# Last step of a fused GNN, attention and mixture-of-experts kernel: where gathered rows lie and when they are added, and how output tiles are stored

## What is computed

```python
topk_p, topk_i = jax.lax.top_k(probs, K)            # K = 2 of E = 8 experts for each row
dispatch = order[:, :capacity]                      # 97 rows for each expert
xg = xf[dispatch]
gate = jax.nn.silu(jnp.einsum('ech,ehi->eci', xg, rg))
up = jnp.einsum('ech,ehi->eci', xg, ru)
eout = jnp.einsum('eci,eih->ech', gate * up, rd)
w = jnp.take_along_axis(wdense.T, dispatch, axis=1)
contrib = eout * (w * valid)[..., None]
routed = jnp.zeros_like(xf).at[dispatch.reshape(-1)].add(contrib.reshape(-1, h))
shared = jax.nn.silu(x @ sg) * (x @ su) @ sd        # inner width 8192
return shared + SCALE * routed.reshape(b, s, h)
```

## Time and profile before

| what | us |
|---|---|
| median of three timed runs | 2904.63 (2904.53 to 2905.37) |
| the profiled execution | 2901.85 |
| its span, first to last instruction | 2900.1 |
| TensorE busy | 2848.7 (98%) |
| VectorE busy | 2232.1 (77%) |
| ScalarE busy | 1498.0 (52%) |
| GpSimd busy | 54.9 (2%) |
| mean granted TensorE clock | 0.993 |

### The profile page before, as it was taken

How to read it: one execution, slowest core, us unless ns; L and a number is a source line. 1 busy time by engine, 2 the same in 40 slices (tenths; PEclk the granted TensorE clock), 3 DMA queues, 4 the chain that set the end, 5 groups by cost and what they waited for, 6 DMA issues and landing times.

```text
span 2900.1 us, 43188 instructions
## 1 busy us (share of the span) xinstructions
PE 2848.7 (98%) x16148; PEld 2403.3 (83%) x16148; DVE 2232.1 (77%) x2724; ACT 1498.0 (52%) x1950; POOL 54.9 (2%) x73
## 2 busy tenths in 40 slices
PE   8999999899999999999999999999999999999997
PEld 8997899878888888888888888888888888888876
DVE  7835334888888888888888888888888888888886
ACT  7722222555555555555555555555555555555562
POOL 0100000000000000000000000000000000000001
PEclk9999999999999999999999999999999999999998
DMA  3010111366666666666666666666666666666684
GB/s 111 29 67 30 59 59 45 101 228 220 217 226 220 219 219 227 220 219 217 227 220 219 219 226 219 219 218 227 220 219 218 226 221 218 220 227 220 218 294 144
DMA packets 265789, 549.18 MB, mean 189 GB/s; under 512 B 16412, under 2 KB 82204, under 8 KB 265437
## 3 DMA queue, kind: packets, MB, share of 16 engines
q1 hardware_dynamic: 261626, 532.20, 54.1%
q0 software_dynamic: 3936, 14.06, 1.5%
HBM read 537.49 MB, written 8.70 MB: 188 GB/s over the span
## 4 chain that ended last, share of the span: by engine, by line
PE 93%; DVE 4%; ACT 1%; issue 1%; DMA 0%; SPq 0%; DVEq 0%; ACTq 0%
PE ps L1818 26%; PE ps L1822 26%; PE ps L1821 26%; PE ps L1558 3%; PE ps L1615 2%; PE ps L1613 2%; PE ps L1614 2%; PE ps L1673 2%; PE ps L1598 1%; DVE c_lo L1355 1%; PE ps L1865 1%; PE ps L1711 1%; PE ps L1709 1%; PE ps L1710 1%; DVE resid L1345 0%
## 5 line engine op out<-in xcount | busy, mean ns | idle before, releaser
L1355 DVE TENSOR_TENSOR c_lo<-raw,c_hi 128x1024 fp32r<-128x1024 f32 x832 | 985.4, 1220 | 100.7 <-ACT c_hi L764 100.4
L764 ACT CAST c_hi<-raw 128x1024 fp32r<-128x1024 f32 x832 | 863.2, 1050 | 155.1 <-PE ps L1822 152.3
L1818 PE MATMUL ps<-tok_hi,c_hi 128*128 128x314 f32 x1792 | 553.1, 309 | 8.3 <-DVE tok_lo L1247 6.4
L1822 PE MATMUL ps<-tok_hi,c_lo 128*128 128x314 f32 x1792 | 552.0, 308 | 0.0
L1821 PE MATMUL ps<-tok_lo,c_hi 128*128 128x314 f32 x1792 | 552.0, 308 | 0.0
L1818 PE MATMUL ps<-c_hi,xgT_hi 128*97 128x512 f32 x1024 | 403.6, 394 | 0.8 <-DVE xgT_lo L1412 0.8
L1822 PE MATMUL ps<-c_hi,xgT_lo 128*97 128x512 f32 x1024 | 403.2, 394 | 0.0
L1821 PE MATMUL ps<-c_lo,xgT_hi 128*97 128x512 f32 x1024 | 402.3, 393 | 0.0
L1419 DVE TENSOR_TENSOR resid<-ps,resid 125x512 f32<-125x512 f32 x320 | 218.7, 686 | 180.5 <-PE ps L1822 180.4
L1818 PEld LDWEIGHTS ps<-tok_hi,c_hi 128*128 128x128 f32 x1792 | 339.6, 189 | 11.4 <-issue 7.2
L1821 PEld LDWEIGHTS ps<-tok_lo,c_hi 128*128 128x128 f32 x1792 | 340.0, 190 | 1.4
(11 more groups left out here) (244 smaller groups left out, 3958.6 us busy)
## 6 DMA issues: line engine op xcount, KB each, us to landing
raw<-in_L_ffn_rg SPq DMA_DIRECT2D x256, 512.0 KB, 4.7
raw<-in_L_ffn_ru SPq DMA_DIRECT2D x256, 512.0 KB, 4.7
raw<-in_L_ffn_rd SPq DMA_DIRECT2D x256, 512.0 KB, 6.2
raw<-in_L_ffn_sg SPq DMA_DIRECT2D x64, 512.0 KB, 4.5
raw<-in_L_ffn_su SPq DMA_DIRECT2D x64, 512.0 KB, 5.4
raw<-in_L_ffn_sd SPq DMA_DIRECT2D x64, 512.0 KB, 5.6
wl<-in_L_mix_w_qkv SPq DMA_DIRECT2D x6, 2048.0 KB, 7.8
wl<-in_L_gnn_W SPq DMA_DIRECT2D x2, 2048.0 KB, 29.5
```

Of the source, the lines that this page charges most:

```text
L764: nc.scalar.copy(c_hi[u % RING][:], raw_at_(q, r)[:]).then_inc(sem("hi_done"), 1 + (U - UNITS) * (u == UNITS - 1))
L1355: V.tensor_tensor(c_lo[u % RING][:], raw_at_(q, r)[:], c_hi[u % RING][:].bitcast(F32), ALU.subtract).then_inc(sem("lo_done"), 1 + (U - UNI ...
L1818: m = MM(out_, l_hi, r_hi, start=first, stop=False, skip_group_check=skip)
L1822: return MM(out_, l_lo, r_hi, start=False, stop=last, skip_group_check=skip)
```

## The change

It does four things, all in the last step or behind it. (1) The gathered rows of tiles 2 to 4 go to six of the raw weight buffers, and GpSimd waits for the split that reads each buffer last (`lo_done`) and no longer for `unit_used`. (2) On VectorE `routed_add` moves into `factors()`, ahead of the splits of S1, A22 and S4. (3) The adds of gathered rows are taken one by one: (0,0) stands ahead of `shared_inner(0)`, (0,1) behind it, tiles 1 and 2 ahead of `shared_up(1)`, and tiles 3 and 4 between the shared adds, ahead of n = 2, 4, 5 and 6. (4) Each output tile leaves as two DMAs, of 112 and 13 rows; the last tile besides in two halves of 512 columns.

```diff
--- before.py
+++ after.py
@@ -321,10 +321,9 @@
     assert here() <= early_at
 
 
-    tok_at = raw_at + RAW * 4096
-    got_at = [eout_at, r_h_at, hT_at, xgT_at]
-    for b in (B11, T3, T2):
-        got_at += [tok_at + b * 8 * 4 * HW, tok_at + b * 8 * 4 * HW + 4 * 4 * HW]
+    last_raw = [raw_at + (((Q - 1) * BLK + b) % RAW) * 4096 for b in range(LAST.b0 - 2, LAST.b0 + 4)]
+    freed, factor = last_raw[:2], last_raw[2:]
+    got_at = [eout_at, r_h_at, hT_at, xgT_at] + freed + [factor[r] for r in (R_A11, R_A22, R_A21, R_A12)]
     got = [[place(f"got{c}_{t}", [P, D], F32, at=got_at[2 * t + c]) for t in range(NT)] for c in range(2)]
 
     def rw_half(i):
@@ -481,12 +480,18 @@
                 step(e, q)
         for q in range(Q):
             step(E - 1, q, LAST if q == Q - 1 else STEP)
-        for t in range(NT):
+        SPLIT = (slice(0, GROWS), slice(GROWS, TP))
+        for t in range(NT - 1):
 
             sp.wait_ge(sem("sd_added"), count(E - 1, Q - 1, 2 * NT, 2 * t + 2 + ONE))
-            sp.dma_start(out_t[t], resid[:, t, :]).then_inc(sem("out_stored"), 16)
-        sp.wait_ge(sem("out_stored"), 16 * NT)
-
+            for rows in SPLIT:
+                sp.dma_start(out_t[t, rows], resid[rows, t, :]).then_inc(sem("out_stored"), 16)
+        for half in range(2):
+            c = slice(half * HALF, (half + 1) * HALF)
+            sp.wait_ge(sem("sd_added"), count(E - 1, Q - 1, 2 * NT, 2 * (NT - 1) + half + 1 + ONE))
+            for rows in SPLIT:
+                sp.dma_start(out_t[NT - 1, rows, c], resid[rows, NT - 1, c]).then_inc(sem("out_stored"), 16)
+        sp.wait_ge(sem("out_stored"), 2 * 16 * (NT + 1))
 
     @block.gpsimd
     def _(pool):
@@ -567,9 +572,11 @@
         pool.dma_start(eout_d[E * CAP:(E + 1) * CAP, :], eout[:]).then_inc(sem("eout_stored"), 16)
         pool.wait_ge(sem("eout_stored"), 16 * (E + 1))
         for t in range(NT):
-            if t >= 2:
-                pool.wait_ge(sem("unit_used"), count(E - 1, Q - 1, U, LAST.s + t - 1 + USED0))
             for c in range(2):
+                if t >= 2:
+                    last = (LAST.s - 2, LAST.s - 1, LAST.s + F_S1, LAST.s + F_A22, LAST.s + F_S4,
+                            LAST.s + F_S4)[2 * (t - 2) + c]
+                    pool.wait_ge(sem("lo_done"), count(E - 1, Q - 1, U, U + last + 1))
                 nc.gpsimd.indirect_dma_start(
                     out=got[c][t][:], out_offset=None, in_=eout_d,
                     in_offset=bass.IndirectOffsetOnAxis(ap=pos_u[:, c, t:t + 1], axis=0)).then_inc(
@@ -1337,13 +1344,11 @@
                 r = eout[:, half * HALF:(half + 1) * HALF]
                 V.tensor_tensor(r, PS[R0 + half][0:CAP, :], r, ALU.add).then_inc(sem("rd_added"), 1)
 
-        def choices_add(t0, t1):
-
-            for t in range(t0, t1):
-                for c in range(2):
-                    dve.wait_ge(sem(f"g_in{c}_{t}"), 16)
-                    link(V.scalar_tensor_tensor(out=resid[:, t, :], in0=got[c][t][0:TP, :], scalar=wts[:, c, t:t + 1],
-                                                in1=resid[:, t, :], op0=ALU.mult, op1=ALU.add))
+        def choice_add(t, c):
+
+            dve.wait_ge(sem(f"g_in{c}_{t}"), 16)
+            link(V.scalar_tensor_tensor(out=resid[:, t, :], in0=got[c][t][0:TP, :], scalar=wts[:, c, t:t + 1],
+                                        in1=resid[:, t, :], op0=ALU.mult, op1=ALU.add))
 
         def step(e, q, order=STEP):
             def lo(u):
@@ -1358,7 +1363,7 @@
             def sums(i):
                 factor_sum(e, q, order, i)
 
-            def factors():
+            def factors(between=None):
 
                 sums(F_S3)
                 lo(order.s + F_A11)
@@ -1369,6 +1374,8 @@
                 lo(order.s + F_S2)
                 lo(order.s + F_A12)
                 sums(F_S4)
+                if between:
+                    between()
                 lo(order.s + F_S1)
                 lo(order.s + F_A22)
                 lo(order.s + F_S4)
@@ -1435,19 +1442,21 @@
                 routed_inner(1)
                 lo(23)
                 turned_lo(1)
-                factors()
-                routed_add(count(e, q, U, order.rd + 8 + USED0), cleared)
+                factors(lambda: routed_add(count(e, q, U, order.rd + 8 + USED0), cleared))
                 shared_up(0)
+                choice_add(0, 0)
                 shared_inner(0)
-                choices_add(0, 1)
+                choice_add(0, 1)
                 lo(31)
                 lo(32)
-                choices_add(1, 2)
+                for t in (1, 2):
+                    for c in range(2):
+                        choice_add(t, c)
                 shared_up(1)
                 shared_inner(1)
                 for n in range(2 * NT):
-                    if n % 2 == 0 and n >= 4:
-                        choices_add(n // 2, n // 2 + 1)
+                    if n in (2, 4, 5, 6):
+                        choice_add(*((3, 0), (3, 1), (4, 0), (4, 1))[(2, 4, 5, 6).index(n)])
                     shared_add(n)
                 return
             if order is FIRST:
```

## The result

The changed kernel takes 2887.83 us in the median of six runs (2886.5 to 2889.31), the kernel before 2904.58 (2903.06 to 2905.46). The ratio is 0.9943, 95% interval 0.9933 to 0.9952: 16.8 us less. The forecast was 2886.0, with a range of 2883 to 2891.5. The profiled execution took 2887.84 us, its span 2886.1.

A forecast was written before the change was run, and what follows sets the result against it. The slow output drain was taken to set the end, hiding VectorE's late last sum. Last sum 8.6 us earlier plus faster stores moves the span from 2900.1 to 2881.5; 2904.63 - 18.6 = 2886.0 us, range 2883 to 2891.5.

The forecast's parts named there:

- Drain by five engines, end set by it: Run's end: output stores drain at 114 GB/s, share 0.31 (5 of 16 engines), hiding VectorE's finish by 13.6 us.
- routed_add for nothing, gathers 7.17 us earlier: Last step: the routed adds fit in VectorE's 2.47 us of idle time; everything on POOL's queue moves 7.17 us forward.
- VectorE's order: Last step: adds laid out on VectorE, last sum at 2877.9 instead of 2886.5; TensorE's gap 0.4 us, full clock.
- The term that I had at 8.6 us: End of VectorE's work: last sum ready 8.6 us earlier, 2886.5 to 2877.9.
- The tail: After the last sum: final 1.02 MB at 277 GB/s takes 3.7 us, plus 0.8; end 2882.0, taken as 2881.5.
- The distance carried over: Whole run: the timed median 2904.63 lies 2.8 us above the profiled 2901.85; this distance was kept unchanged.
- Rival A: Saturated DMA stretch, last step: ScalarE late again, end 1.9 to 4.5 us later, 2888 to 2890.5; chance 0.16.
- Rival B: Final stores: last three 13-row pieces run behind the 112-row ones, end 2.1 us later, 2888.1; chance 0.05.
- C: Last step's gathers: rows land as late as now, only the drain's rate helps, 11 us less, 2893.6; chance 0.06.
- D: Final stores: 114 GB/s limits the written side, not five engines; 4.6 us less, 2900.0; chance 0.04.
- E: First gathered add: each microsecond its rows come beyond 2849.7 delays the end by one; slower, 2911; chance 0.02.

## Why the prediction was right, point by point

- *Drain by five engines, end set by it.* Right: the share was 0.31 before and 0.32 with the stores of 125 put back, 5 of 16 engines by estimate, and the two kernels that change only the store show that it set the end: tail 13.59 to 3.60 us, and back to 17.27.
- *routed_add for nothing, gathers 7.17 us earlier.* Right: no split moved (ahead of the first one 1.14 us idle are left), and GpSimd's store was issued 2.72 us behind the start of the factor sum against 9.90 before, 7.18 us earlier. Putting it back cost 8.1 us.
- *VectorE's order.* The last add 38.87 us behind the factor sum by my layout (2877.9 - 2839.03), 38.93 measured; TensorE's gap 0.31 against 0.4, the clock behind it 1.00. The term that I had at 8.6 us was 8.55 (47.48 - 38.93).
- *The tail.* This term of the sum was mis-sized: 3.6 us by my number (2881.5 - 2877.9), 5.26 in the profiled execution, 4.73 to 4.75 in three others. The working had 3.7 us for the last 1.02 MB at 277 GB/s, and 0.8 behind, which gives 2882.0; I then took 2881.5, half a microsecond less, for no reason in a row. The data themselves took from about 2880.5 to 2885.3 in the changed kernel, at 255 GB/s up to 2884.5 and at 33 and less behind. The rate of a lone tile (the stores of y) was used for two tiles in a row, one behind the other; the order with tile 3 first, in which tile 4 leaves alone, has 3.64. In the profiled execution these 1.7 us are nearly the whole distance from 2886.0 to 2887.83; with the usual tail of 4.75 they would have been 1.1.
- *The distance carried over.* I added the 2.8 us between the median and the profiled execution of the kernel before unchanged. The profile of the changed kernel took 2887.84 us, its median, and its last factor sum started 2.88 us later than in the profile before. So the carry was right: the profile before was a quick one in its untouched part.
- *Rival A* came true in part: ScalarE is late in all nine profiled executions with ten early gathers, by 1.1 to 3.3 us at worst, mostly hidden and worth 1.8 us in one. I had it at 0.16 as a case of its own; it is rather a spread on every run. The clock did not fall with it: behind the 2.15 us of standing still it was granted at 1.00, behind 6.54 us (routed_add late) at 0.50.
- *Rival B* (small pieces dear) fell. With tile 3's data out of the way the tail is 3.6 us with four pieces, two of them of 13 rows, and the last tile stored whole, with one small piece less, has 4.69 against 4.73 to 4.75.
- *Rivals C, D and E* fell: C by GpSimd's store, 7.18 us earlier, and the 0.68 us that the first rows were awaited, D by the windows at a share of 0.84. E's sum is 0.2 us short (18.6 + 5.8 + 4.4 is 28.8), which changes nothing. E's mechanism is real where the rows are late, as the late routed_add shows.

## What to carry to other kernels

Read the DMA share in the last windows before the arithmetic. Here it stood flat at 0.31 with stores of 125 rows, 5 of 16 engines by estimate, and changing nothing but the pieces to 112 + 13 rows, with the last tile in halves, took 10.1 us off the end; the share of such stores in the changed kernel was 0.84. When two limits lie over each other at the end, each alone shows less than its worth (10.1 and 4.7 us, against 16.9 together), so price them together. And price the last transfers with what still stands ahead of them in the queue, not by one that ran alone: the tail was 3.64 us with tile 3 gone, and 5.26 and 4.75 behind its data in the changed kernel's two executions.

## What the hardware showed that I had not expected

ScalarE starts up to 3.3 us late on waits that TensorE has satisfied; every case seen behind the last factor sum fell while GpSimd's indirect gathers ran, and with the last six of them left out none was left. The profile names some of these waits "remote". SP's issue of four stores takes 1.82 us where the tile before is nearly gone and 2.85 us with half a megabyte ahead of them. And the untouched part of the kernel ends at 2839.0 to 2845.4 us, a scatter of 6 us under every single profile; only times counted from a fixed point of the last step could tell effects of 1 us.
